# Layer 1 experts: constant weight addresses for every second token tile, looked-up addresses for the others

## The reference, cut to what matters

```
probs = softmax(x @ gate_weight.T)                 # 1024 x 64
top_val, top_idx = top_k(probs, 8)                 # 8 experts per token
top_val = top_val / sum(top_val)
mapping = ...                                      # rarely used experts are merged into a similar one
flat_e = mapping[top_idx].reshape(-1)              # the first 4 of a token's 8 keep their expert
order = argsort(flat_e); xs = x[order // 8]        # rows grouped by expert
gate, up = split(ragged_dot(xs, gate_up_proj), 2)  # 256 -> 2 x 96, the weights of the row's expert
y = ragged_dot(silu(gate) * up, down_proj)         # 96 -> 256
out = sum over the token's 8 rows of weight * y
```

## Time and profile before

| | us |
|---|---|
| median of 3 runs | 1802.05 |
| the three runs | 1802.05, 1797.75, 1803.91 |
| the profiled execution, device time | 1810.02 |
| its span from first to last instruction | 1808.2 |
| PE busy, of the span | 1600.4 (89%) |
| tile loop, first to last `turn_act` | 549.5 to 749.8 |

### The profile page before, as it was taken

How to read it: one execution, slowest core, us unless ns; L and a number is a source line. 1 busy time by engine, 2 the same in 40 slices (tenths; PEclk the granted TensorE clock), 3 DMA queues, 4 the chain that set the end, 5 groups by cost and what they waited for, 6 DMA issues and landing times. The chain is left out here.

```text
span 1808.2 us, 27168 instructions
## 1 busy us (share of the span) xinstructions
PE 1600.4 (89%) x8877; PEld 1263.2 (70%) x8878; DVE 1002.3 (55%) x2336; ACT 803.6 (44%) x1766; POOL 413.5 (23%) x420
## 2 busy tenths in 40 slices
PE   4999996997739999887878988989999999999897
PEld 3777655774627888665644876867888888888665
DVE  2277336243554544312656354566777777777576
ACT  3577353343324455300775443344544445544443
POOL 2400011112056665464100212231101111011000
PEclk9999995998859999855999998997999999999999
DMA  3000030133424555433000115330000000000100
GB/s 122 13 18 1 1 149 9 35 90 85 199 106 146 167 168 165 128 93 108 15 1 9 44 36 131 90 96 18 18 1 17 17 17 17 0 17 0 46 0 23
DMA packets 55628, 109.34 MB, mean 60 GB/s; under 512 B 9905, under 2 KB 37425, under 8 KB 53914
## 3 DMA queue, kind: packets, MB, share of 16 engines
q1 hardware_dynamic: 45330, 82.10, 14.3%
q0 software_dynamic: 9168, 25.05, 5.1%
q10 hardware_dynamic: 1040, 1.05, 0.2%
HBM read 89.39 MB, written 18.78 MB: 60 GB/s over the span
## 5 line engine op out<-in xcount | busy, mean ns | idle before, releaser
L1681 POOL DMA_INDIRECT h_modulated<-l1f_rows,ln_rstd x127 | 121.0, 953 | 82.2 <-PE bank L1748 55.7
L2808 ACT ACTIVATE l_mem<-bank 128x129 f32<-128x129 f32 x240 | 66.2, 279 | 158.7 <-PE bank L2658 158.7
L2545 POOL COPY l_sg<-l_keys 128x512 f32<-128x512 f32 x32 | 24.3, 760 | 370.4 <-DVE l_keys L2918 370.4
L2670 PE MATMUL bank<-l_mem,l_sg 128*128 128x129 f32 x480 | 102.6, 318 | 2.5 <-ACT l_mem L2808 0.5
L2658 PE MATMUL bank<-l_dr,l_nkt 128*128 128x129 f32 x480 | 98.4, 296 | 7.2 <-DVE l_dr L2963 6.7
L1761 PE MATMUL bank<-l1f_up,l1f_wt 128*128 x508 | 104.6, 329 | 0.0
L1804 PE MATMUL bank<-l1f_wt,ln_square 128*128 128x128 f32 x256 | 72.8, 448 | 23.2 <-DMA ln_square<-l1f_y_rows,l1f_back_at 15.8
L1966 DVE COPY l1f_wt<-bank 128x256 f32<-128x256 f32 x127 | 53.9, 425 | 65.3 <-PE bank L1748 48.9
L2670 PEld LDWEIGHTS bank<-l_mem,l_sg 128*128 128x128 f32 x480 | 73.3, 195 | 22.7 <-ACT l_mem L2808 5.3
L2963 DVE SCALAR_TENSOR_TENSOR l_dr<-bank,l_inv,l_v 128x128 f32<-128x128 f32 x240 | 84.3, 351 | 8.5
L1775 PE MATMUL bank<-l1f_down,ln_rstd 96*128 x254 | 87.5, 426 | 1.3 <-ACT ln_rstd L1847 0.9
(11 more groups left out here) (614 smaller groups left out, 4368.4 us busy)
## 6 DMA issues: line engine op xcount, KB each, us to landing
l1f_y_rows<-h_modulated SPq DMA_DIRECT2D x127, 128.0 KB
l1f_up<-in_l1f_up SPq DMA_DIRECT2D x8, 1536.0 KB
l_w<-in_l_w SPq DMA_DIRECT2D x9, 768.0 KB, 4.4
wmod<-in_wmod SPq DMA_DIRECT2D x4, 1536.0 KB, 10.1
l1f_down<-in_l1f_down SPq DMA_DIRECT2D x4, 1536.0 KB, 21.9
l2e_w<-in_l2f_win SPq DMA_DIRECT2D x14, 256.0 KB, 2.8
l_w<-in_l_wqk SPq DMA_DIRECT2D x8, 256.0 KB, 2.7
l0m_w<-in_l0f_win SPq DMA_DIRECT2D x8, 256.0 KB, 2.7
```

The costliest lines, as they stand in the source:

```text
L1681: pool.indirect_dma_start(xg[:, i % GETS], None, table, bass.IndirectOffsetOnAxis(ap=listing[:, i:i + 1], axis=0)).then_inc(got[i % GETS], 16)
L2670: pe.matmul(k.bank[:, READ + a, 0:W1], sg[:, a, n // 2, at:at + 2, :], mem[:, a, n % 2, 0:W1], start=True, stop=True).then_inc(s["read_rea ...
L2808: act.activation(mem[:, a, (n + 1) % 2, 0:W1], k.bank[:, MEM + a, 0:W1], ACT.Identity).then_inc(s["mem_copied"], 1)
```

## The change

The tiles are numbered anew. Tile e, for e = 0 to 63, holds the first 128 rows of expert e, so its weights stand at an address that is known when the program is built. The other 63 tiles (64 to 126) hold the rows from the 129th on of whichever experts have them, and look their expert up as before. The loop takes the two kinds in turn: `ORDER` is 0, 64, 1, 65, ..., 62, 126, 63. All loops still run over i = 0 to 126; `ORDER[i]` only picks the column of `listing`, the DRAM rows for the result, and the weights. `load_owner` issues nothing for a constant tile.

The routing's arithmetic changes with it: the number of further tiles of an expert is (max(n, 1) - 1) >> 7, and the place of a row depends on whether its rank is below 128. That takes one more table (`first_base`, made by POOL) and three more DVE instructions.

```diff
+    MORE = TILES - E
+    ORDER = [i // 2 + (E if i % 2 else 0) for i in range(2 * MORE)] + list(range(MORE, E))
...
-                    sp.dma_start(y_rows[tile(i)], yb[:, i % PUTS]).then_inc(y_stored[i % PUTS], 16)
+                    sp.dma_start(y_rows[tile(ORDER[i])], yb[:, i % PUTS]).then_inc(y_stored[i % PUTS], 16)
...
+                step.link(pool, pool.iota(first_base[:], pattern=[[-P, E]], base=END, channel_multiplier=0,
+                                          allow_small_or_imprecise_dtypes=True))
...
-                        ap=listing[:, i:i + 1], axis=0)).then_inc(got[i % GETS], 16)
+                        ap=listing[:, ORDER[i]:ORDER[i] + 1], axis=0)).then_inc(got[i % GETS], 16)
...
                 def load_owner(i):
-                    owner_reg[i] = pe.value_load(owner_of[0:1, i:i + 1], min_val=0, max_val=E - 1)
+                    if ORDER[i] >= E:
+                        at = ORDER[i] - E
+                        owner_reg[i] = pe.value_load(owner_of[0:1, at:at + 1], min_val=0, max_val=E - 1)
+
+                def of_owner(w, i):
+                    if ORDER[i] >= E:
+                        return w[:, bass.ds(owner_reg[i], 1)]
+                    return w[:, ORDER[i]:ORDER[i] + 1]
...
-                                         up[:, bass.ds(owner_reg[i], 1), b, :], start=(b == 0), stop=(b == DB - 1))
+                                         of_owner(up, i)[:, :, b, :], start=(b == 0), stop=(b == DB - 1))
...
-                    pe.matmul(k.bank[:, Y + i % 2, 0:D], at[:, i % 2], experts.down[:, bass.ds(owner_reg.pop(i), 1), :],
+                    pe.matmul(k.bank[:, Y + i % 2, 0:D], at[:, i % 2], of_owner(experts.down, i),
...
-                step.link(dve, dve.tensor_scalar(whole[:], k.bank[:, TOTALS, 0:E], P - 1.0, None, ALU.add))
+                step.link(dve, dve.tensor_scalar(whole[:], k.bank[:, TOTALS, 0:E], 1.0, -1.0, ALU.max, ALU.add))
...
-                step.link(dve, dve.tensor_scalar(base[:], base[:], -float(P), float(END), ALU.mult, ALU.add))
-                step.link(dve, dve.tensor_tensor(p[:], over(base[:], TT), k.bank[:, PREFIX, :].rearrange(
-                    "p (t e) -> p t e", t=TT), ALU.subtract))
+                step.link(dve, dve.tensor_scalar(base[:], base[:], -float(P), float(END - (E - 1) * P), ALU.mult,
+                                                 ALU.add))
+                step.link(dve, dve.tensor_tensor(base[:], base[:], first_base[:], ALU.subtract))
+                ranks = k.bank[:, PREFIX, :].rearrange("p (t e) -> p t e", t=TT)
+                step.link(dve, dve.scalar_tensor_tensor(p[:], ranks, float(P), over(base[:], TT), ALU.is_ge, ALU.mult))
+                step.link(dve, dve.tensor_tensor(p[:], p[:], over(first_base[:], TT), ALU.add))
+                step.link(dve, dve.tensor_tensor(p[:], p[:], ranks, ALU.subtract))
```

More of the change, by code:

```diff
@@ L1605, in l1_experts @@
         base = sb("base", [P, E])
+        first_base = sb("first_base", [P, E])
         owner = sb("owner", [P, 1])
```

## The result

The changed kernel takes 1777.61 us (median of 4 runs, 1776.1 to 1780.21), the kernel before beside it 1800.28 us (4 runs, 1797.75 to 1803.91). The ratio is 0.9874, with a 95% interval of 0.9851 to 0.9897: 22.7 us less.

The account below looks back on a forecast made before the run. The prediction took PE's sequencer list to bound the tile loop. Loop -19.3 us and routing +1.7 us gave -17.6 us, taken from the 1802.05 us median: 1784.5 us, range 1778 to 1797 us for 8 in 10.

Parts of the forecast that it names:

- What bounds the kernel: Tile loop: PE's sequencer list of lookup, register operations, matmuls and waits is as long as the tile.
- The base: Whole kernel: the forecast difference of -17.6 us was applied to the three runs' median, 1802.05 us.
- The profiled execution: Whole kernel: the profile took 1810.02 us, 8 us above the median; its rows gave the prices and the difference carried over.
- Rival C: Tile loop: PE's signals to other engines come late more often, 1.46 us each; at one in six tiles 1815 us; chance 0.05.
- The loop's term: Tile loop: 126 periods shorten from 1.583 to 1.43 us, a gain of 19.3 us.
- the margin of 0.28 us: Looked-up tiles: slack at a 1.41 us period for DVE's late row copy, before operation and weight load of some 0.1 each.
- The list's split: PE's sequencer per tile: lookup 0.7 us, three register operations about 0.1 each, matmuls and waits 0.5 us.
- The routing stage: DVE's chain ahead of the gathers: three more instructions cost +1.7 us, the three-operand form nothing extra.
- Gathers and stores at nothing: POOL's gathers and SP's stores: same number and size, only DRAM order changes, so no cost; POOL has 0.16 us to spare.
- Rival A: Tile loop: looked-up tiles stay at 1.58 us, constant ones 1.41, half the gain, 1793.3 us; chance 0.16.
- Rival B: Tile loop: the DVE and ACT loop sets 1.58 us, or the queue already hides lookups; no gain, 1803.7 us; chance 0.12.
- The rule on the queue: Tile loop: PE's 64-instruction queue would already hide a 0.7 us lookup behind 1.41 us of matmuls, so halving lookups gains nothing.

Follow-up runs that it names:

- the undisturbed pair of profiles: Profiles without late signals: the kernel before, unchanged, profiled again (loop 195.2 us), and the changed kernel (178.2 us).
- the second profile: The kernel before, unchanged, profiled again in a later group of runs: 1796.44 us (10 runs), ratio 1.0003; loop 195.2 us.
- the one with two lookups: The changed kernel with each lookup done twice in a row: 1790.04 us (10 runs), ratio 0.9969 against the kernel before.

## Why the prediction was right, and where it failed

**What bounds the kernel: right.** The sequencer's list was longer than the matmuls. Taking out the lookup alone, the address alone, or half of both brings the tile to PE's 1.416 us wherever no gather is late; putting lookups back brings 1.50 and 1.80.

**The base: the step that failed.** The forecast was 1784.5 us and 1777.6 came, just outside the range. The sum was carried over to 1802.05 us, the median of three runs. With many more runs the kernel before has 1796.41 us (18 runs), 1794.34 (12) and 1796.53 (11). The forecast's own difference on that base is 1796.4 - 17.6 = 1778.8 us, and the changed kernel's three medians are 1777.61, 1778.49 and 1780.06. The difference was sound: by the later two comparisons it was 17.9 and 16.5 us where 17.6 was forecast (the undisturbed pair of profiles accounts for 15.3 of it). The range allowed the three runs 2 to 4 us round their median, and gave their median no error of its own, though it was 5.6 us high: of the 51 later runs of the kernel before, only three reach it. The 22.7 us measured at first hold the same error, since three of their four runs of before are the sum's own. Whether those four (all at 1797.75 us or more, where 15 of the 51 are) were high by chance or by some condition of that group of runs stays open; the changed kernel beside them wasn't high.

**The profiled execution: read as if it were the kernel.** It took 1810.02 us, 8 us more than the median, and the prediction carried that difference over without asking where the 8 us were. The rows that it used held more than that: with the late signals went 4.9 us in the loop and 10 us on the way back, and without these 14.9 the profile would be at 1795.1 us, beside the 1796.4 of the later runs and not beside 1802.05. So 1.583 us per tile held some 0.02 us that no edit of the list could remove in a usual execution, and the earlier trace rows, on which Rival C rested, was a stall of that execution alone. So was most of the "issue" ahead of `turn_act` that it took from the earlier trace rows; the part ahead of the down products was the kernel's.

**The loop's term: two errors that nearly cancel.** 1.43 us was taken for the tile after; it was 1.417, since no copy was late, and the 0.02 added for late copies weren't needed (the margin of 0.28 us worked out from the earlier trace rows used a late signal). 1.583 was taken for before; it was 1.561 in the second profile. 126 x (1.561 - 1.417) = 18.1 us by these, 17.0 by first and last `turn_act`, 19.3 in the sum. The matmul time of 1.41 us from one tile was right to 0.01.

**The list's split: wrong, without consequence.** The prediction gave matmuls and waits 0.5 us, the lookup 0.7 and the register operations 0.3. The runs give some 0.82, 0.61 and 0.13. The start times in the earlier trace rows were read as the price of the piece that starts there; but the matmuls that the sequencer hands over have no row in that view, and they fall into the gaps between the rows. For the changed kernel both splits are below PE's time (1.0 or 1.19 against 1.41), so it did no harm here. For more lookups it did: the forecasts of 1.42 and 1.70 us were made with it, and 1.50 and 1.80 came.

**The routing stage: right**, +1.71 us for +1.7, and nothing for the three-operand form. **Gathers and stores at nothing: right**; POOL kept up, with gathers 1.41 us apart and 0.47 us of idle time before each near 642 us.

**Rival A fell** (no two-step pattern), though the tiles that look up are slow when they stand together (1.564). **Rival B fell**: neither the loop over DVE and ACT nor anything else but the list set the old period, as removing nothing but lookups, or nothing but register addresses, ends it (1.416 us). **Rival C fell**: no late signal in any kernel with a denser stream. What makes the late signals stays open: one profile in 14 shows them, and no edit brought them back.

**The rule on the queue.** The kernel whose steps have lists of some 2.04 and 0.95 us, the one with two lookups, and the changed one show that a queue smooths single steps, and that a list longer than the matmuls on average is not hidden. The Trainium skill ("TensorE: Matmul & The Clock Gate", Architectural detail) gives PE a queue of 64 instructions; read as "a lookup is hidden", it fails in the kernel before (1.561 us) and is met in the changed one (1.417). The same page (Wait — 56ns, not 53.3ns?) puts the sequencer's microcode at about 62 ns per matmul where hardware decode is off. Nine matmuls would be 0.56 us by that, an estimate; the runs give 0.82 with the weight loads and waits in it, and none of them separates these.

## What to carry over

Where an engine's idle time ends at "issue", or loads start late behind each other while it looks 100% busy, compare the time of its sequencer's list with the time of its work, as means over a few steps: what can be made constant, made cheaper or put next to a short step counts until the list is the shorter one, and nothing after. Take the price of a sequencer's operation from two kernels that differ in their number of it and are both bound by the list, not from the spacing of its rows. Look at the single periods of a stretch before its mean is taken for a price: one late gather in 40 tiles added 0.01 us. When a profile's time stands above the median of the runs, find out which of its rows are the excess before a sum is built on them, and give a base from three runs an uncertainty of its own.

## What the runs showed of the hardware

A lookup of a value with bounds costs PE's sequencer 0.61 us (two lookups against three), twice the 0.30 us of the TENSOR_LOAD in its row. By the estimates above the three register operations of a tile's register-addressed operands cost some 0.13 us and its nine matmuls with loads and waits some 0.82 us, all unseen in PE's busy time. Without the comparison with its bounds a lookup is short enough that M + L + R is at most PE's 1.417 us, so it costs some 0.47 us at most. PE's signals to DVE and POOL can come late through a whole execution: 55 of 127 copies started over 0.2 us after the modelled end of their transposes, and none in 13 other profiles, and that execution was 15 us longer in the loop and on the way back. And the same kernel's median moved from 1794.3 to 1800.3 us between groups of runs, a third of the gain that was to be measured.
